# Drive terms one step ahead in a Mamba attention, and a new order of work in a relative attention

## The reference

```python
u = silu(conv(u) + conv_b)
dbc = u @ xproj_w.T                              # 64 dt ranks, 16 B, 16 C
dt = softplus(dbc[..., :64] @ dt_w.T + dt_b)     # 256 channels
dA = exp(dt[..., None] * A)                      # 16 states for each channel
dBu = (dt * u)[..., None] * Bm[:, :, None, :]
h = dA_t * h + dBu_t                             # a scan over the time steps
y = sum over states of h * C, plus u * D
out = (y * silu(z)) @ out_w.T
```

## Time and profile before

| | before |
|---|---|
| device time, median of 3 | 3718.3 us (3717.51 to 3730.32) |
| profiled execution: its time, its span | 3722.02 us, 3720.3 us |
| busy in the span: PE, DVE, ACT, POOL | 3346.1, 2413.3, 1881.9, 1719.1 us |
| relative attention, about 1330 to 2010 us: PE, DVE busy | 644.92 of 680 us, 420.80 |
| last attention, about 2584 to 3461 us: PE, DVE busy | 829.80 of 877 us, 773.82 |
| TensorE clock granted in these two stages | 0.99 and 1.00 |

### The profile page before, as it was taken

One profiled execution on the slowest core, in us unless ns is written; L12 is line 12 of the kernel. 1 busy time (PEld: TensorE's weight loads), 2 busy tenths in 40 slices (PEclk: granted clock), 3 DMA queues, 4 the chain that ended last, 5 costly groups with the idle time before them and its releaser, 6 DMA issues. The chain is left out here.

```text
span 3720.3 us, 70277 instructions
## 1 busy us (share of the span) xinstructions
PE 3346.1 (90%) x24448; PEld 2239.0 (60%) x24448; DVE 2413.3 (65%) x5383; ACT 1881.9 (51%) x5083; POOL 1719.1 (46%) x1885
## 2 busy tenths in 40 slices
PE   6889997869999989999997999997999999999676
PEld 3666653647777756666664444444677777777565
DVE  4888843556666646666664344447888888889325
ACT  4767755466666634444545000006766676666123
POOL 3665522337777733333331000002767767767664
PEclk8999998889999989999999999997999999999887
DMA  4889830030000000000001787652553222222423
GB/s 133 226 225 232 229 92 11 1 78 1 1 2 2 1 1 1 1 2 2 1 2 47 155 153 149 154 125 74 118 123 89 79 75 81 78 76 85 132 83 113
DMA packets 312552, 300.56 MB, mean 81 GB/s; under 512 B 72137, under 2 KB 227721, under 8 KB 311946
## 3 DMA queue, kind: packets, MB, share of 16 engines
q1 hardware_dynamic: 307594, 286.58, 31.4%
q0 software_dynamic: 4608, 9.48, 0.8%
HBM read 237.45 MB, written 58.53 MB: 80 GB/s over the span
## 5 line engine op out<-in xcount | busy, mean ns | idle before, releaser
L2414 DVE TENSOR_TENSOR_SCAN a_h<-a_dA,a_dBu_psum 128x512 f32<-128x512 f32 x512 | 595.5, 1204 | 101.9 <-issue 70.4
L2299 POOL TENSOR_TENSOR a_h<-a_h,main_g 128x512 f32<-128x512 f32 x256 | 383.2, 1499 | 238.4 <-DVE a_h L2414 173.8
L1247 POOL TENSOR_SCALAR a_probs<-a_probs,a_row_inv 128x128 f32<-128x128 f32 (+1 forms) x512 | 380.0, 763 | 164.1 <-DVE a_row_inv L1210 164.1
L1713 DVE SCALAR_TENSOR_TENSOR m_hidden<-m_h_psum,m_gate_spread 128x512 f32<-128x512 f32 x256 | 176.6, 691 | 265.0 <-PE m_h_psum L1651 252.2
L179 POOL TENSOR_TENSOR main_g<-main_g,main_s 128x512 f32<-128x512 f32 x28 | 44.0, 1605 | 650.4 <-ACT main_g L161 650.4
L1998 PE MATMUL a_dBu_psum<-a_B_diag,a_dt_u_turned 64*128 64x128 f32 x4096 | 323.5, 290 | 23.3 <-DVE a_h L2414 22.4
L1516 POOL TENSOR_TENSOR r_position_q<-r_turned_q 128x512 f32<-128x512 f32 x128 | 159.7, 1269 | 389.2 <-DVE r_turned_q L1561 389.2
L1998 PEld LDWEIGHTS a_dBu_psum<-a_B_diag,a_dt_u_turned 64*128 64x128 f32 x4096 | 260.6, 188 | 81.3 <-issue 77.5
L1473 ACT ACTIVATE r_probs<-r_logits_psum,r_neg_max 128x256 f32<-128x256 f32 x512 | 235.0, 475 | 139.9 <-DVE r_neg_max L1567 139.9
L1152 ACT ACTIVATE a_probs<-a_logits,a_neg_max 128x128 f32<-128x128 f32 (+1 forms) x512 | 226.7, 446 | 128.1 <-DVE a_neg_max L1196 128.1
L1567 DVE TENSOR_REDUCE r_neg_max<-r_logits_psum 128x2 f32<-128x512 f32 x256 | 164.9, 686 | 184.1 <-PE r_logits_psum L1383 184.1
(11 more groups left out here) (516 smaller groups left out, 7558.2 us busy)
## 6 DMA issues: line engine op xcount, KB each, us to landing
m_gate_spread<-m_gate_rows SPq DMA_DIRECT2D x64, 1024.0 KB, 8.3
main_g<-a_b_c_rows SPq DMA_DIRECT2D x256, 256.0 KB, 3.2
a_band_rows<-main_g SPq DMA_DIRECT2D x64, 512.0 KB, 4.2
a_B<-a_band_rows SPq DMA_DIRECT2D x192, 128.0 KB, 3.4
a_A<-a_band_rows SPq DMA_DIRECT2D x192, 128.0 KB, 3.2
f_x_expert<-f_x_rows SPq DMA_DIRECT2D x16, 322.5 KB, 2.9
f_x_rows<-a_zero SPq DMA_DIRECT2D x16, 320.0 KB, 5.0
f_stage_w<-L_ffn_up_weights SPq DMA_DIRECT2D x9, 512.0 KB, 7.2
```

The costliest lines, as they stand in the source:

```text
L1247: ins = nc.gpsimd.tensor_scalar(pr[:, h % NPR, tile[t]], pr[:, h % NPR, tile[t]], rinv[:, p % NST, q:q + 1], None, ALU.mult)
L2299: tt(h[:, r, :, :], h[:, r, :, :], Cs[:, g % NCS, :, :], ALU.mult).then_inc(hc_pool, 1)
L2414: nc.vector.tensor_tensor_scan(flat, dA[:, M % NDA, q, k, :, :].rearrange("p n t -> p (n t)"), db[:, 2 * (g % 2) + k, :], 0.0, ALU.mult, A ...
```

## The change

**Last attention.** A step is now one channel half k for both sequences (k = g % 2), where it was one sequence for both halves. The low projection's columns are stored in blocks of 64 time steps, the sequences alternating (`mixed`, `blocks`), so that rows 0 to 63 of a turned tile belong to sequence 0 and rows 64 to 127 to sequence 1. Each row tile then writes only into the bank of its own sequence, and `half_mm`, the second half of `drive`, is gone. All 8 matmuls of `drive(g + 1)` now stand in iteration g: the addends are complete a step ahead. `sum_states`, `gate`, `decay` and `read_c` follow the new meaning of a step: a tile of C now serves two steps, `decay` waits for one step less at k = 0, and the rows of B and C go out in two DMAs (`store`).

**Relative attention.** The same instructions in another order on TensorE, VectorE and ScalarE.

```diff
@@ relative_attention, tensor
                     if p < NQ:
                         add_position(p, 0)
+                        add_position(p, 1)
                     for what, b in beside(p):
                         make(what, b, p)
                     if 1 <= p <= NQ:
                         transpose(p - 1, 1)
-                    if p < NQ:
-                        add_position(p, 1)
-                    if 1 <= p <= NQ:
-                        transpose(p - 1, 2)
                     if p + 2 < NQ:
                         position(p + 2, p)
                     if 1 <= p <= NQ:
-                        transpose(p - 1, 3)
+                        transpose(p - 1, 2)
                     if 2 <= p < NQ + 2:
                         weigh(p - 2)
+                    if 1 <= p <= NQ:
+                        transpose(p - 1, 3)
@@ relative_attention, scalar
+                    if p < NQ:
+                        exps(p, 2)
                     if 1 <= p <= NQ:
                         turn(p - 1, 2)
                     if p < NQ:
-                        exps(p, 2)
                         exps(p, 3)
@@ l3_attention, tensor
-                def drive(g, second):
+                def drive(g):
                     U, j = g // STEPS, g % STEPS
-                    M, q = g // 2, j % 2
-                    if second:
-                        pe.wait_ge(half_mm, 2 * (g + 1))
-                    else:
-                        if j == 0:
-                            pe.wait_ge(dtuT_sb, 2 * U + 2)
-                        pe.wait_ge(diag_sb, M + 1)
-                        if g >= 2:
-                            pe.wait_ge(scanned, NK * (g - 1))
-                    for tc in range(TC):
-                        for half in range(2):
-                            k = 1 - half if second else half
...
+                    M, k = g // 2, j % 2
+                    if j == 0:
+                        pe.wait_ge(dtuT_sb, 2 * U + 2)
+                    pe.wait_ge(diag_sb, M + 1)
+                    if g >= 2:
+                        pe.wait_ge(scanned, 2 * (g - 1))
+                    for b in range(T // HALF):
+                        for q in range(2):
+                            rows = slice(HALF * q, HALF * (q + 1))
+                            dst = db[:, 2 * (g % 2) + q, :].rearrange("p (n t) -> p n t", n=2)
+                            ins = mm(dst[:, :, b * HALF:(b + 1) * HALF], dtuT[U % 2][rows, b // TC, b % TC, k * P:(k + 1) * P],
+                                     diag[rows, M % NDIAG, b, :, rows], start=True, stop=True, tile_position=(HALF * q, 0),
+                                     skip_group_check=True)
...
-                    drive(g, True)
                     if g < LAST:
-                        drive(g + 1, False)
+                        drive(g + 1)
@@ l3_attention, sync
                     sp.wait_ge(low_sb, N + 1)
-                    sp.dma_start(scratch[N % 2].rearrange("q n t -> n q t"), by_seq(low[DR + NS:, :])).then_inc(bc_st, 16)
-                    sp.wait_ge(bc_st, 16 * (N + 1))
+                    for q in range(2):
+                        sp.dma_start(scratch[N % 2, q].rearrange("n (b i) -> n b i", i=HALF),
+                                     mixed(low[DR + NS:, :])[:, q]).then_inc(bc_st, 16)
+                    sp.wait_ge(bc_st, 32 * (N + 1))
...
-                    if g >= NCS:
-                        sp.wait_ge(hc_dve, g - NCS + 1)
-                        sp.wait_ge(hc_pool, g - NCS + 1)
+                    if r >= NCS:
+                        sp.wait_ge((hc_dve, hc_pool)[q], 2 * (M - NCS // 2) + 2)
@@ l3_attention, gpsimd
-                    tt(dtu[N % 2][:, k, :], dt[N % 2][:, k, :], u[:, k, :], ALU.mult).then_inc(dtu_sb, 1)
+                    tt(mixed(dtu[N % 2][:, k, :]), blocks(dt[N % 2][:, k, :]), blocks(u[:, k, :]), ALU.mult).then_inc(dtu_sb, 1)
```

More of the change, by code:

```diff
@@ L1590, in _ @@
                     if p < NQ:
-                        maximum(p, 2)
                         maximum(p, 3)
-                    if 1 <= p <= NQ:
-                        turn(p - 1, 3)
                     if p + 2 < NQ:
@@ L1597, in _ @@
                             rotate(p + 2, i)
+                    if 1 <= p <= NQ:
+                        turn(p - 1, 3)
         s.barrier()
@@ L2018, in sum_states @@
-                    for k in range(NK):
-                        pe.wait_ge((hc_dve, hc_pool)[k], g + 1)
+                        pe.wait_ge(ud_sb, 2 * U + k + 1)
+                        for i in range(2 * TC):
+                            mm(yT[:, k, i * P:(i + 1) * P], ud[:, k, i * P:(i + 1) * P], c["ident"][:], start=i == 0, stop=False,
+                               is_transpose=True, skip_group_check=True)
+                    for q in range(2):
+                        pe.wait_ge((hc_dve, hc_pool)[q], g + 1)
```

109 lines of the change are left out of this document (55 added, 54 removed).

## The result

The changed kernel takes **3680.6 us** as the median of 4 runs (3675.4 to 3681.6), beside 3718.8 us for the kernel before on the same chip (4 runs, 3717.5 to 3730.3): a ratio of 0.9888 [0.9866, 0.9909]. That is 38 us less. The forecast was 3664, 54 us less, with a range that holds the result.

The account below looks back on a forecast made before the run. TensorE was taken as the fullest engine in both stages, in the last attention blocking in turn with VectorE. From 3722.0 us, less 39 (last attention) and 16 (relative attention), 3667; adjusted to the runs' median, 3664, range 3636 to 3694.

Parts of the forecast that it names:

- The seesaw: Last attention: TensorE waits for a scan after short steps, VectorE for TensorE's addends behind long projections, each in turn.
- The 2.6 us that I counted in a unit: Last attention: TensorE's time lost per steady unit to waits for scans and split bursts; all of it was to go.
- After the change step g + 1's addends are ready when scan g is under way: Last attention: the step of lead suffices; VectorE is not held up unless TensorE comes 2 us late.
- a thing that would not be seen: Last attention, sign: VectorE's idle time ahead of scans is not named by bursts that just ended.
- Relative attention, -16: Relative attention: only r = 0 gains, 1.42 us; other steps lose 0.05 to 0.17; four steps 40.87 against 41.90, -16 us.
- the forecast 2.32 us: Relative attention: from transpose 2 to the next content logits, over ScalarE's copy and its last two exponentials, 2.32 us.
- I take nothing: Last attention: the new block order costs GpSimd nothing; 0.3 us more per product would have cost 9 us in 15 units.
- 52.5: Last attention: forecast length in us of one unit after the change, from 55.10 before.
- -39: Last attention: forecast gain in us, 15 units times 2.6; the last unit gains nothing.
- If dt*u comes later than today: Last attention, sign of a wrong prediction: GpSimd's product dt*u comes later than in the kernel before.
- the third rival: Last attention: another wait, GpSimd's product ahead of `sum_states` or dA, takes the freed time; only -16 left, 3702; chance 0.08.
- the rival of +279 us: Last attention: the two row tiles no longer run side by side, each burst about 1.09 us longer, 3940; chance 0.04.

Follow-up runs that it names:

- e3: Kernel before with only the last attention's change, but each whole burst of addends in its own step, not a step ahead: 3690.7 us, 0.9913.
- e10: Changed last attention, VectorE making one GpSimd product a unit, bursts in their own step; relative attention as before except turned sums moved at r = 0: 3690.0 us, 0.9834.
- e1: Kernel before with the new order of the relative attention alone: 3711.0 us, 0.9963.
- e6: Kernel before with only the turned sums at r = 0 moved behind the second burst and their copy behind the third maximum: 3700.8 us, 0.9939.
- e4: Kernel before with GpSimd's product dt*u taken in the changed kernel's blocks of 64 elements: 3725.0 us, 1.0006.
- e8: Changed kernel with VectorE's product with C over 4 of 512 elements only, so output is incomplete: 3646.2 us in one run.
- e7: Changed kernel with VectorE instead of GpSimd making the second product with C in step j = 10 of each unit: 3659.3 us, 0.9827.

## Why the prediction was right, and where it was off

- **The seesaw ends, for TensorE.** Right for the engine that sets the pace: bursts are whole, and in the full units no wait for a scan is left. The 2.6 us that I counted in a unit are all gone, and 55.10 less 2.6 plus the 0.62 of the third point is 53.1, measured 53.17. The reason was wrong. "After the change step g + 1's addends are ready when scan g is under way" was my argument, with the step that VectorE "is not held up". The trace of after contradicts it: two scans in a unit stand 0.70 and 1.39 us before a burst that has just ended, which I had named as a thing that would not be seen. And e3 takes the lead away and keeps the gain, as e10 does in the steady units with GpSimd's waits gone. What is left is the unsplit burst. That the total held all the same is luck in part: the held-up engine was not the one that binds.
- **Relative attention, -16.** Right: -15.1, the four steps 41.02 for 40.87, and from transpose 2 (1710.51) to the logits (1712.83) the forecast 2.32 us. `position` waited 0.58 - 0.17 = 0.41 at r = 0, where I had 0.39. e1 and e6 bear the split out: r = 0 gains, the others pay. By the rule of the Trainium skill that the prediction cites (TensorEngine Tiling (Array Packing), Key Properties), that a change of tiling mode drains TensorE, there would have been 13 us more. The joined burst needs one change less, and from transpose 2 to the logits the step is still as long as the chain over ScalarE: the trace goes with the chain.
- **"I take nothing" for GpSimd.** This is the term that failed in size. I looked for a cost in the layout, and e4 shows that there is none in this product. But I held GpSimd's stretch around dt*u fixed while moving everything beside it. After the change VectorE stands 0.24 us before a scan there where it stood 1.01 (3099.11 and 3130.54), and its products fall beside GpSimd's. The waits grow from 0.99 and 0.34 to 1.18, 0.16 and 0.48 us, and the stretch from 6.81 to 7.43: 0.62 of the 0.67 us by which the unit misses 52.5. In 15 units that is the 10 us between -39 and -29.4. That VectorE's products lengthen GpSimd's is shown by e8, that the waits hang on GpSimd's queue by e7, and that a shift in time alone moves them by this much by e3, with 6.87 us for the same instructions. The rows also tell where the 0.62 lies. Up to the start of GpSimd's two products at 3098.20 the stretch has lost 0.09 us (4.99 from the burst at 3093.21, before 4.90 from 3125.56): the product behind dt*u takes 0.46 more, but the select behind it as much less (1.09 for 1.55). The other 0.53 is the first of these two products, with VectorE's of 3098.21 beside it. "If dt*u comes later than today" was a sign of being wrong, and it came: this is the third rival, in small.
- **The other terms.** The bursts did not grow (286 ns a matmul at L1999, 1.09 us a burst), so the rival of +279 us is out. C's reads and the second DMA of `store` appear in no wait of TensorE's or VectorE's. Of the 16 us between forecast and result (54 and 38), 10 are the term above, 1 is the relative attention, 3 the tail that differs between executions, and 2 stay unassigned.

## What to carry to other kernels

When a wait is taken away, walk the next engine in line as it will run then, not as it ran before: its instructions may be the same and still take longer, since others now run beside them. Before reordering a whole step to remove one wait, move the waiting piece alone: here that gave 22 us where the reorder gave 15. And where a buffer is filled in two parts, each released by a wait of its own, first fill it in one part, before adding lead: here that was the whole gain. An engine named in a wait may have been done long before; the code says what the instruction needs, and the row that ends just ahead of it says what it got.

## What the runs showed of the hardware

- VectorE's products of two SBUF operands and GpSimd's instructions take turns: 1.27 us becomes 1.73 on GpSimd, 0.66 becomes 1.45 on VectorE, and 0.13 becomes 1.30 for 4 elements. VectorE's scans, which read their addends from PSUM, stay at 1.20 us beside GpSimd's work (1183 to 1222 ns over 512 of them).
- A product in blocks of 64 elements is as fast on GpSimd as one in a row: 1496 and 1495 ns.
